# A wait for the preceding gather put before each indirect gather in three stages of a graph network kernel

## The reference, cut to what matters

```python
h = relu(layernorm(x)); x = x + spmm(spmm(h))          # edge_weight * h[src], summed by dst, twice
h = relu(layernorm(x)); x = x + gcn(h @ W)             # norm * h[src], summed by dst, and the node itself
h = relu(layernorm(x)); x = x + mlp(h + sum(h[src]))   # summed by dst
h = relu(layernorm(x)); x = x + update(h, sum(message(h[src], h[dst], edge_attr)))
```

## Time and profile before

| what | us |
|---|---|
| median of three runs | 4624.67 |
| lowest and highest run | 4622.48, 4624.89 |
| profiled execution, span | 5754.7 |
| busy in it: PE, DVE, ACT, POOL | 3759.0, 3033.3, 2016.3, 3313.7 |
| first source stage, first gather to last DVE read of `ga` | 2131.7 to 3015.2 |
| second source stage, the same | 3068.8 to 3962.3 |
| last stage, the same | 4002.5 to 5572.8 |

### The profile page before, as it was taken

One profiled execution on the slowest core, in us unless ns is written; L12 is line 12 of the kernel. 1 busy time (PEld: TensorE's weight loads), 2 busy tenths in 40 slices (PEclk: granted clock), 3 DMA queues, 4 the chain that ended last, 5 costly groups with the idle time before them and its releaser, 6 DMA issues. The chain is left out here.

```text
span 5754.7 us, 60611 instructions
## 1 busy us (share of the span) xinstructions
PE 3759.0 (65%) x18706; PEld 3006.2 (52%) x18706; DVE 3033.3 (53%) x7288; ACT 2016.3 (35%) x5132; POOL 3313.7 (58%) x2843
## 2 busy tenths in 40 slices
PE   3776666676999975565556777763566655666665
PEld 2544444446898964444445555553454444455454
DVE  4644444455556546665665766755454434455442
ACT  2444444451111113443444444431233333333332
POOL 4888888887888874444332554553444554445544
PEclk7776666675555557887888777875778877777787
DMA  8333333334444432222222333333121111121110
GB/s 293 51 51 51 51 51 51 51 42 73 87 81 87 87 40 82 78 93 79 96 77 75 108 125 123 112 107 130 54 91 55 59 57 57 54 91 55 60 54 21
DMA packets 335488, 452.10 MB, mean 79 GB/s; under 512 B 208111, under 2 KB 233301, under 8 KB 334740
## 3 DMA queue, kind: packets, MB, share of 16 engines
q1 hardware_dynamic: 159268, 361.69, 17.8%
q0 software_dynamic: 176000, 87.72, 12.5%
HBM read 258.41 MB, written 225.53 MB: 84 GB/s over the span
## 5 line engine op out<-in xcount | busy, mean ns | idle before, releaser
L929 POOL DMA_INDIRECT ga<-table,isl x784 | 783.9, 1000 | 278.1 <-issue 231.3
L1059 POOL DMA_INDIRECT out_x<-acc,osl x392 | 430.0, 1097 | 755.6 <-DVEq L80 640.4
L997 POOL DMA_INDIRECT xu<-acc,osl x392 | 625.1, 1595 | 144.6 <-issue 103.1
L1205 PE MATMUL tp<-xw,cc 128*128 128x394 f32 x784 | 411.5, 623 | 345.8 <-DVE cc L2011 215.4
L1242 PE MATMUL tp<-us,wide 128*128 128x64 f32 x1568 | 416.8, 422 | 87.4 <-DVE us L2139 49.2
L929 POOL DMA_INDIRECT ga<-xu,isl x392 | 394.0, 1005 | 121.5 <-issue 116.5
L1205 PEld LDWEIGHTS tp<-xw,cc 128*128 128x128 f32 x784 | 141.5, 220 | 603.1 <-issue 325.4
L1093 PE MATMUL mm<-ident,wide 128*128 128x128 f32 x1176 | 213.1, 343 | 355.6 <-DVE wide L2218 275.7
L1242 PEld LDWEIGHTS tp<-us,wide 128*128 128x128 f32 x1568 | 380.0, 332 | 92.2 <-DVE us L2139 49.4
L1255 PE MATMUL tp<-acc,wide 128*128 128x64 f32 x1560 | 423.3, 427 | 0.8
L1093 PEld LDWEIGHTS mm<-ident,wide 128*128 128x128 f32 x1176 | 180.0, 182 | 406.1 <-issue 323.2
(11 more groups left out here) (378 smaller groups left out, 9513.8 us busy)
## 6 DMA issues: line engine op xcount, KB each, us to landing
wide<-xu SPq DMA_DIRECT2D x84, 448.0 KB
zx<-key_rows SPq DMA_DIRECT2D x28, 896.0 KB
out_x<-wide SPq DMA_DIRECT2D x56, 448.0 KB, 3.4
table<-acc SPq DMA_DIRECT2D x56, 448.0 KB, 2.5
xf<-xs SPq DMA_DIRECT2D x56, 448.0 KB
wide<-table SPq DMA_DIRECT2D x56, 448.0 KB
xu<-in_x SPq DMA_DIRECT2D x25, 1000.0 KB
hop_even<-zeros SPq DMA_DIRECT2D x1, 12544.0 KB
```

The lines of the kernel that those rows point to most:

```text
L929: nc.gpsimd.indirect_dma_start(o[:, g, :], None, table, bass.IndirectOffsetOnAxis(idx[:, g:g + 1], 0)).then_inc(s, 16)
L997: nc.gpsimd.indirect_dma_start(xu, bass.IndirectOffsetOnAxis(osl[b][:, g:g + 1], 0), acc[b][:, g, :], None, compute_op=ALU.add).then_inc(f ...
L1059: nc.gpsimd.indirect_dma_start(out, bass.IndirectOffsetOnAxis(osl[b][:, g:g + 1], 0), acc[b][:, g, :], None, bounds_check=nodes_max, oob_i ...
L1205: f.key_row.raise_by(nc.tensor.matmul(tp[1][:, at:at + KEYS], reach[:, g * P:g * P + P], key_steps, start=True, stop=True), ("g", b, g))
```

## The change

A helper `gather_singly` is added on POOL. It issues the same 14 gathers, but before each it waits until the semaphore of the unit shows that all gathers before it have landed: 16 for each of this unit, on top of `landed`, which is 16 times 14 for each earlier step. Both source stages and the last stage call it in place of `gather`. Nothing else changes: the same transfers, buffers and order.

```diff
+            def gather_singly(o, table, idx, s, landed):
+
+                for g in range(G):
+                    if g or landed:
+                        after.wait_ge(s, landed + 16 * g)
+                    gather(o, table, idx, s, (g,))
+
             after.wait_ge(s_node, 1)
             base = 0
...
                         after.wait_ge(s_slot, base + 2 * i + n + 1)
-                        gather(ga[b], table, isl[b], f.got[b])
+                        gather_singly(ga[b], table, isl[b], f.got[b], 16 * G * i)
...
                         after.wait_ge(s_slot, base + b + 1)
-                    gather(ga[b], tables[1], isl[b], tt.got_a[b])
+                    gather_singly(ga[b], tables[1], isl[b], tt.got_a[b], 16 * G * i)
```

## The result

The changed kernel takes 6237.33 us (median, 6234.02 to 6241.47) against 4624.78 of the kernel before beside it, a ratio of 1.3486 with the interval 1.3467 to 1.3505: 1612.6 us slower. Predicted were 5907 us and a range from 5290 to 6420. The direction and the range held; the forecast was 330 us short.

A forecast was written before the change was run, and what follows sets the result against it. DVE's passes were taken to bound the kernel, covering the gathers until serial ones at 2.65 us make POOL set the pace: 436 + 361 + 445 + 40 = +1282 on 4624.7 gives 5907 us, range 5290 to 6420.

The forecast's parts named there:

- What bounds the kernel: All three stages: POOL waits for DVE, whose pass covers the gathers; slower gathers are free until 28 fill a pass.
- Subtracting the remote waits: DVE's waits for PE's products, 267.5, 176.8 and 543.6 us by stage, taken as absent from the runs.
- the runs are like the profile: Rival, chance 0.10: dead time is real or evenly spread, last stage stays hidden; 5017 us, or 4940 if the profile shrinks evenly.
- The second source stage before: Second source stage of the unchanged kernel in the runs: 792.6 - 176.8 = 615.8 us.
- The price of a gather: Each serial gather: 2.35 us landing + 0.3 to the next start = 2.65, against 1.25 now; bounds 2.1 and 4.3.
- the first wait costs nothing: Each unit's first wait is free, as its gathers landed a step earlier; a unit was still priced 14 x 2.65 + 0.5.
- Landing is slow: Rival, chance 0.12: gathers wait behind SP's 448 KB tiles, 3.1 us each; together +1784, about 6410 us.
- The last stage: Last stage: a POOL step becomes 114.5 us, hidden in the profile's 123.5 but not the runs' 74.1: +445.
- The rule on landing: Trainium skill's SWDGE path, about 2.0 us plus bytes: a gather lands after 2.08 us, ending the sum at about 5600.
- The signs: Changed profile: starts 2.65 us apart, source passes 75, last-stage steps near 123, no source-stage remote waits, span near 6150.
- Faster: Rival, chance 0.02: serial gathers below 1.5 us stay hidden and SP's transfers run freer; at most 35 us gained, 4590.

The follow-up runs named there:

- the kernels that left the stage alone: The waits in one stage only, against the kernel before: first source stage 5140.36 us, second source stage 5140.97 us, last stage 5194.78 us.
- one pause in 14 gathers: Kernel before plus waits only before each unit's first and eighth gather: all three stages 5539.20 us (0.9515) and 5427.36 (0.9426), source stages alone 5491.92 (0.9538).
- pairs: All three stages wait, but only before every second gather, so two are in flight; against the kernel before: 5356.97 us, ratio 1.1591.

## Why the prediction was right, and where it was not

All lengths in us; those of before come from the kernels that left the stage alone, on the first kind of chip.

| stretch | before, predicted | measured | after, predicted | measured | cost, predicted | measured |
|---|---|---|---|---|---|---|
| first source stage | 616.0 | 618.5 | 1052 | 1137.5 | +436 | +519 |
| second source stage | 615.8 | 572.4 | 977 | 1095.2 | +361 | +523 |
| last stage with its start | 74.1 a step | 75.5 | 114.5 a step | 114.9 | +485 | +556 |

For the last row the reads from the second step on give 1415.5 - 906.1 = +509, and the stretch before them, from the end of the second source stage, 169.5 - 123.0 = +46.5. The three make +1598 of 1612.6, and behind the last read another +9.

- **What bounds the kernel: right.** POOL waited for DVE and the gathers were hidden by its pass, until 28 of them fill it. In the source stages the pass went from 44 to 81 us and more, POOL never idles for DVE.
- **Subtracting the remote waits: right in its numbers, wrong in its reason.** It gave 616.0 and 74.1 where the runs have 618.5 and 75.5. But "this dead time exists in the profiled execution alone" is wrong. It exists in each execution on one kind of chip, and the forecast held since the runs were made on the other. That was luck: on the second kind the change adds 572 us, less than half of the 1282 forecast. The rival "the runs are like the profile" is what happens there: it adds 392.5 us by its account, and 572 were measured.
- **The second source stage before: 43 us too long.** Not all of its dead time is in the two rows subtracted (138.0 + 38.8); the rest passed as natural pace. That is 43 of the 162 us missing there; the other 118 are the price, below.
- **The price of a gather: the mis-sized term.** 2.65 us was right for a quiet one (2.70 in the timeline). The mean, wait and busy time together, is 709.2 / 358 + 1.02 = 3.00 us in the first source stage and 756.4 / 361 + 1.01 = 3.11 in the second. A unit is 13 such gathers and one that doesn't wait, which with the copy starts 1.42 us behind the one before: 13 x 3.00 + 1.42 = 40.4, and 28 x 40.4 = 1132 against 1137.5 measured. The text said that the first wait costs nothing, and then priced 14 waits; that slip took 1.7 us per unit too much and hid part of the error. "Landing is slow" had the right mechanism, a gather that waits behind SP's tiles, and nearly the right price (3.1) but only a 0.12 chance. I had put it aside since quick landings lie beside dense traffic too. They do, but a serial stream meets all of the traffic, and a mean is made by the late ones.
- **The last stage: right.** It isn't hidden in the runs; the reason is stronger than the one given, for POOL had been the bound there already. Scatters issued later cost nothing of their own.
- **The rule on landing.** The quickest landing in this trace takes 2.3 us and the median 2.5. The Trainium skill (DMA: Bandwidth & Descriptors, section Anatomy of one DMA) gives, as an estimate, 2.08 by its SWDGE path for a DMA of this size; the trace does not agree, and the forecast of about 5600 made with it falls 640 us short. No run here varies the bytes of a gather, so none shows how much of the time is fixed cost.
- **The signs.** Starts 2.7 apart, POOL's waits turned round, DVE waiting for `ga`, no remote waits in the source stages: all seen. "Steps still near 123 in the last stage" and "span near 6150" were not: 114.9 and 6232.2, because this profile came from the first kind of chip. On the second kind (6327.54) the step is 120.4 and the span 6336.4.
- **Faster** didn't come about for the change on either kind of chip. But on the second kind the question it asked, whether spacing the gathers frees others, has the answer yes: one pause in 14 gathers gains 5 to 6%, one after each gather loses more than it frees.

## What to carry to other kernels

A small gather on POOL's queue takes 1.25 us of the queue when it is issued behind another, and its whole landing plus 0.3, here 2.7 us in quiet and 3.0 to 3.1 beside 448 KB tiles, once it has to be waited for; price a serial stream at its mean beside the traffic, not at the quick landing. Count the waits that hold the queue, not the gathers: pairs have 0.46 of them and cost 0.46 of the full change. And where a profile is a quarter longer than the runs shown with it, ask first whether both come from the same kind of chip (the mean granted clock of the same kernel, 0.72 against 0.78 here, was a sign of it), before a theory is built on the gap.

## What was unexpected in the hardware

The same kernel takes 4621 us on one chip and 5756 to 5813 (medians) on another, in every run. The difference is dead time of DVE and PE beside back-to-back indirect DMAs of POOL: up to 49.8 us in one wait, shorter by 16.9 us when the burst is shorter by 17.5, and absent in the source stages when each gather is waited for. With each gather waited for, the kernel takes 6237 us on the one and 6328 on the other, so that nearly all of the difference between the chips is gone. Of the 90 us left, 66 lie in the last stage, where the scatters are still back to back and DVE's remote waits sum to 231.7 us.
